# GpSimd normalises attention probabilities in four per-head pieces and takes their low parts in two halves

## The chip, the cores and the metric

The kernel runs on one core of one Trainium2 chip. The metric is the device time of one execution in microseconds (us); lower is better. Engine names as in the profile: PE is TensorE (matmuls), PEld its weight loads, DVE is VectorE, ACT is ScalarE, POOL is GpSimd, SP is SyncE, which here only issues DMAs.

## The reference

One transformer block on 16 independent sequences of 128 tokens and 512 channels: layer norm, cross-attention against a context of 128 positions and 128 channels (16 query heads, 4 key/value heads, rotary embedding, causal mask), a residual, layer norm, and a feed-forward with 4-bit weights and low-rank corrections. Cut to what matters:

```python
q = _rms_norm(q, q_norm_w); k = _rms_norm(k, k_norm_w)        # heads of 32, rotary on both
scores = jnp.einsum('bgnqd,bgkd->bgnqk', qg, k) * scale
scores = jnp.where(causal, scores, -1e+30)
attn = jax.nn.softmax(scores, axis=-1)                         # 16 heads, 128 x 128 each
out = jnp.einsum('bgnqk,bgkd->bgnqd', attn, v) ... @ w_out.T
x = x + out
y1 = ln(x) @ w_up + b_up + ln(x) @ w_up_lora_a @ w_up_lora_b   # 512 -> 2048
y2 = relu(y1) @ w_down + b_down + ...                          # 2048 -> 512
return x + y2
```

## The kernel before, in words

All matrices are held as a high and a low part in float16, and a product is three matmuls (high by high, low by high, high by low). A sequence ("batch" n, 16 of them) goes through: statistics, centring, rotary products (DVE, POOL, ACT), the split of queries and keys, their DMA transposes, scores on PE, and then the softmax in four tiles m = 0 to 3 of four heads each, 128 partitions by 512 columns:

- DVE masks the scores of a tile and takes the row maxima (`mask_and_max`, L1203), ACT takes exponentials and row sums (`exponentials`, L691, L696), and DVE takes the reciprocals of the four row sums (L1111).
- POOL multiplies the tile `pr[:, m]` (four heads of 128 columns) by the four reciprocals `rinv`, one per head and partition, in a single instruction (`probabilities`, L506), and signals `probs`.
- ACT rounds the tile to float16, the high part (L722), and signals `p_high`.
- POOL subtracts the high part from `pr[:, m]` in a single instruction, which gives the low part (`probabilities_low`, L515), and signals `p_low`.
- SP waits for both and issues the DMA transpose of the tile (L409) into `pT`. When all four tiles have landed, PE multiplies by the values (L907), and the output projection follows (L919).

The feed-forward of the batch then runs as four groups up (`feed_forward`, L937) and four parts down (L951). Between them DVE and ACT form `z`, `hid` and its low part (L1132, L756, L1141), and SP transposes them (L417). In the first fifth of the run the 4-bit weights are also unpacked: 32 tiles, scaled mostly by DVE (`dequant`, L1095; five by POOL, L476 and L479), turned on PE (L795, L848), split by ACT (L648) and DVE (L1103).

The order of the instructions on each engine is written out by hand. Time is cut in slots `s`, 264 of them to a batch, and tables `R_...` name the slot of each step for each engine; a step at batch n from 3 on repeats every 264 slots. A slot is no time: within one engine it is only the order, and between engines only semaphores tie. In a steady batch the order on POOL is: `values_low` (L521), `keys` (L489, L490, L493), `value_scales` (L529), probabilities of tiles 0 and 1, low part of tile 0, low part of tile 1, the power for the query and key norms (L498), `y` base (L555), probabilities of tile 2, the power for the second norm (L545), probabilities of tile 3, `cosines` (L538), low parts of tiles 2 and 3. On SP it is: keys, hidden part 0, queries, hidden part 1, probabilities tile 0, hidden parts 2 and 3, second norm (L394), probabilities tile 1, loads of a later batch, probabilities tiles 2 and 3, store.

Who waits for the touched steps: ACT's L722 waits for `probs` of its tile (L719), POOL's L515 for `p_high` (L514), SP's L409 for `p_high` and `p_low` (L405, L406), and DVE's L1203 of the next batch for `p_low` of the same tile (L1198), since it overwrites `pr[:, m]`.

Of the kernel before, what the change touches and what calls it, by code (L numbers as in the profile page):

```python
# [10 lines left out]
ALU = mybir.AluOpType  # L11
# [3 lines left out]
P = 128  # L15
# [92 lines left out]
def build(nc, x, ctx, qw, kw, wo, wuq, wus, bu, wua, wub, wdq, wds, bd, wda, wdb,  # L108
# [3 lines left out]
    HD, NG = 32, 4  # L112
# [16 lines left out]
    with ExitStack() as es:  # L129
# [16 lines left out]
        p3 = big[:, 6144:].bitcast(F16).rearrange("p (m g a t) -> p m g a t", m=NN, g=NG, a=2)  # L146
# [52 lines left out]
        pr = sb("pr", [P, NN, NG, P])  # L199
# [17 lines left out]
        rsum, rinv = sb("rsum", [P, 2, NN * NG]), sb("rinv", [P, 2, NN * NG])  # L217
# [50 lines left out]
        exps, inv_sums, probs = sem("exps"), sem("inv_sums"), sem("probs")  # L268
        sums_scaled, p_high, p_low = sem("sums_scaled"), sem("p_high"), sem("p_low")
# [48 lines left out]
        for s in range(SLOTS):  # L318
            n = at(s, R_VSUM)
            if n is not None:  # L320
                projs_before[n] = len(sums_before)
            n = at(s, R_PROJ)
            if n is not None:
                sums_before[n] = len(projs_before)
        for s in range(SLOTS):
# [5 lines left out]
            for g in range(4):  # L331
                n = at(s, R_UP[g])
# [4 lines left out]
                n = at(s, R_DOWN[g])  # L337
# [10 lines left out]
        def _(sp):  # L348
# [31 lines left out]
            for s in range(SLOTS):  # L380
                n = at(s, R_KTURN)
                if n is not None:
                    sp.wait_ge(k_low, n + 1)
                    sp.wait_ge(k_high, n + 1)
                    if n > 0:
                        sp.wait_ge(scores, 4 * n)
                    sp.dma_start_transpose(kT[:], k3[:].rearrange("p g a d -> p (g a d)")).then_inc(k_turned, 16)
                n = at(s, R_XNTURN)
                if n is not None:
                    sp.wait_ge(xn_high, n + 1)  # L390
                    sp.wait_ge(xn_low, n + 1)
                    if n > 0:
                        sp.wait_ge(up_done, 4 * n)
                    sp.dma_start_transpose(xnT[:], xn_parts[:].rearrange("p a c -> p (a c)")).then_inc(xn2_turned, 16)  # L394
                n = at(s, R_QTURN)
                if n is not None:
                    sp.wait_ge(q_low, n + 1)
                    sp.wait_ge(q_high, n + 1)
                    if n > 0:
                        sp.wait_ge(scores, 4 * n)  # L400
                    sp.dma_start_transpose(qT[:], q3[:].rearrange("p h a d -> p (h a d)")).then_inc(q_turned, 16)  # L401
                for m in range(NN):
                    n = at(s, R_PTURN[m])
                    if n is not None:
                        sp.wait_ge(p_high, 4 * n + m + 1)  # L405
                        sp.wait_ge(p_low, 4 * n + m + 1)  # L406
                        if n > 0:
                            sp.wait_ge(heads_out, n)
                        sp.dma_start_transpose(pT[:, m], p3[:, m].rearrange("p g a t -> p (g a t)")).then_inc(p_turned[m], 16)  # L409
                for g in range(4):  # L410
                    n = at(s, R_X2TURN[g])
                    if n is not None:
                        sp.wait_ge(x2_high, 4 * n + g + 1)
                        sp.wait_ge(x2_low, 4 * n + g + 1)
                        if n > 0:
                            sp.wait_ge(down_done, n)
                        sp.dma_start_transpose(x2T[:, g], hid[:, (4 * n + g) % HID_RING].rearrange("p a h -> p (a h)")).then_inc(x2_turned[g], 16)  # L417
                for g in range(1, 8):
                    if LOAD_AT[g - 1] == s:
                        load_group(g)  # L420
                for i, (parts, rows, moved) in enumerate(((b_up_parts, b_up3, b_up_rows), (b_dn_parts, b_dn3, b_dn_rows))):
                    if LORA_B_ROWS_AT[i] == s:
                        sp.wait_ge(b_high, 2)
                        sp.wait_ge(b_low, 2)
                        sp.wait_ge(lora_rows_empty, 4)
                        for j in range(3):
                            sp.dma_start(rows[R * j:R * j + R],
                                         parts[:, j, :]).then_inc(moved, 16)
                for n in (1, 2, 3):
                    if BATCH_LOAD_AT[n - 1] == s:  # L430
                        load_batch(n)
                if s == LORA_D_LOAD_AT:
                    sp.dma_start(a_nat[:, KC * R:].rearrange("p (g a) -> p g a", a=4 * R), wda_v).then_inc(a_dn_in, 16)
                if s == WO_LOAD_AT:
                    sp.dma_start(wo_raw, wo.rearrange("(j p) c -> p j c", p=P)).then_inc(wout_in, 16)
                if s == ROW_LOAD_AT:
                    sp.dma_start(b_row[:], bu.rearrange("(a n) -> a n", a=1).broadcast_to([P, H])).then_inc(bias_row_in, 16)
                if s == DOWN_BIAS_LOAD_AT:
                    sp.dma_start(bd_bc[:], bd.rearrange("(a n) -> a n", a=1).broadcast_to([P, C])).then_inc(down_bias_in, 16)
                n = at(s, R_STORE)  # L440
                if n is not None:
                    store(n)
                n = at(s, R_LOAD)
                if n is not None and n + RING < B:
                    load_batch(n + RING)
# [4 lines left out]
        def _(pool):  # L450
# [49 lines left out]
            def probabilities(s):  # L500
                for m in range(NN):
                    n = at(s, R_PROBS[m])
                    if n is not None:
                        p = n % 2
                        pool.wait_ge(inv_sums, 4 * n + m + 1)
                        pool.tensor_tensor(pr[:, m], pr[:, m],  # L506
                                           rinv[:, p, 4 * m:4 * m + 4].unsqueeze(2).broadcast_to([P, NG, P]),
                                           ALU.mult).then_inc(probs, 1)

            def probabilities_low(s):  # L510
                for m in range(NN):
                    n = at(s, R_PLOW[m])
                    if n is not None:
                        pool.wait_ge(p_high, 4 * n + m + 1)  # L514
                        pool.tensor_tensor(p3[:, m, :, 1, :], pr[:, m], p3[:, m, :, 0, :], ALU.subtract).then_inc(p_low, 1)  # L515

            def values_low(s):
                n = at(s, R_VLOW)
# [67 lines left out]
        def _(act):  # L586
# [112 lines left out]
            def attention(s):  # L699
                n = at(s, R_SQUARES)  # L700
                if n is not None:
                    act.wait_ge(kv_in[n % RING], 16 * (n // RING + 1))
                    if n >= 2:
                        act.wait_ge(v_summed, n - 1)
                    act.activation(sq_junk[:], kvt[:, n % RING, :], ACT.Square,
                                   accum_out=ssq[:, n % 2:n % 2 + 1]).then_inc(ctx_sq, 1)
                n = at(s, R_KSPLIT)
                if n is not None:
                    act.wait_ge(norms, n + 1)
                    act.wait_ge(k_ready, n + 1)  # L710
                    if n > 0:
                        act.wait_ge(k_turned, 16 * n)
                    act.activation(k3[:, :, 0:2, :], k[:].rearrange("p (g d) -> p g d", d=HD).unsqueeze(2)
                                   .broadcast_to([P, NG, 2, HD]), ACT.Identity,
                                   scale=inv[:, n % 2, 1:2]).then_inc(k_high, 1)
                for m in range(NN):
                    n = at(s, R_PHIGH[m])
                    if n is not None:
                        act.wait_ge(probs, 4 * n + m + 1)  # L719
                        if n > 0:  # L720
                            act.wait_ge(p_turned[m], 16 * n)
                        act.activation(p3[:, m, :, 0, :], pr[:, m], ACT.Copy).then_inc(p_high, 1)  # L722
                n = at(s, R_VSPLIT)
                if n is not None:
                    act.wait_ge(v_scaled, n + 1)
                    if n > 0:
                        act.wait_ge(heads_out, n)
                        act.wait_ge(v_low, n)
                    act.activation(vs[:], kvt[:, n % RING, :], ACT.Identity,
                                   scale=v_scales[:, n % 2, 0:1]).then_inc(v_sized, 1)  # L730
                    act.wait_ge(v_sized, n + 1)
                    act.activation(v3[:, 0, :], vs[:], ACT.Copy).then_inc(v_high, 1)
# [244 lines left out]
        def _(dve):  # L977
# [213 lines left out]
            def mask_and_max(s):  # L1191
                for m in range(NN):
                    n = at(s, R_MASK[m])
                    if n is not None:
                        p = n % 2
                        dve.wait_ge(scores, 4 * n + m + 1)
                        if n > 0:
                            dve.wait_ge(p_low, 4 * n + m - 3)  # L1198
                        if n == 0 and m == 0:
                            dve.wait_ge(consts_in, 16)  # L1200
                        for g in range(NG):
# [127 lines left out]
```

## Time and profile before

| what | value |
|---|---|
| time, median of 3 runs | 485.31 us (483.17 to 486.15) |
| the profiled execution | 484.46 us |
| its span, first to last instruction | 482.7 us |
| PE busy | 443.0 us, 92% |
| DVE busy | 352.0 us, 73% |
| ACT busy | 300.3 us, 62% |
| POOL busy | 282.1 us, 58% |
| L506, 64 instructions of 128x512 | 72.7 us, mean 1137 ns |
| L515, 64 instructions of 128x512 | 80.9 us, mean 1272 ns |
| mean granted TensorE clock | 0.979 of full |

The busy share of an engine is an average over stages with different limits. The profiled execution's own 484.46 us holds 1.8 us outside its span, and is 0.85 us under the median of the three runs.

### The profile page before, as it was taken

To read this page: it belongs to the slowest core of one execution; us is meant where nothing else is said; L and a number is where in the kernel's file an instruction comes from. 1 tells how busy PE (TensorE), PEld (TensorE's weight loads), DVE (VectorE), ACT (ScalarE), POOL (GpSimd) and SP (SyncE) were. 2 spreads that over 40 slices of the span, in tenths; PEclk is the share of its full clock that TensorE was granted. 3 is DMA by queue.
4 is the path that set the end of the run, shared out by engine and by line. 5 is a ranking of instruction groups with operands and counts; after the bars stand their busy time and mean duration, and the time that the engine had idled before them with its cause. 6 is when DMAs were issued, how large, how long until landed. Compare 5 with 4: busy or idle time off the path is not lost.

```text
span 482.7 us, 8285 instructions
## 1 busy us (share of the span) xinstructions
PE 443.0 (92%) x2416; PEld 218.2 (45%) x2416; DVE 352.0 (73%) x1076; ACT 300.3 (62%) x927; POOL 282.1 (58%) x304
## 2 busy tenths in 40 slices
PE   0285869999999999999999999999999999999997
PEld 0164545444444444444444444444444445444443
DVE  3899998979879786868686877778777856534341
ACT  1698978878858675757575757666675856422120
POOL 5477767685859574848384747576657745451100
PEclk9996879999999999999999999999999999999999
DMA  8679769789777858887867777897697777474422
GB/s 224 215 245 175 189 206 209 114 167 141 160 121 137 168 109 160 135 171 114 171 130 155 134 158 132 169 132 161 122 135 163 118 153 110 91 125 93 88 56 74
DMA packets 207740, 70.36 MB, mean 146 GB/s; under 512 B 196880, under 2 KB 200096, under 8 KB 207056
## 3 DMA queue, kind: packets, MB, share of 16 engines
q1 hardware_dynamic: 206864, 69.35, 72.7%
q8 instruction: 19, 0.31, 0.3%
q10 hardware_dynamic: 752, 0.34, 0.3%
q0 software_dynamic: 80, 0.16, 0.2%
q14 instruction: 25, 0.20, 0.1%
HBM read 17.15 MB, written 4.19 MB: 44 GB/s over the span
## 4 chain that ended last, share of the span: by engine, by line
PE 78%; DVE 1%; DMA 1%; SPq 0%; issue 0%
PE ff L951 33%; PE ff L937 33%; PE tb L919 8%; PE sb L891 2%; PE tb L907 2%; DMA x<-hid 1%; SPq L401 0%; PE tb L877 0%; DVE t_sin L1171 0%; DVE pr L1203 0%; DVE y L1253 0%; DVE stats L1184 0%; DVE x L1181 0%; DVE q L1212 0%; DVE q L1118 0%
## 5 line engine op out<-in xcount | busy, mean ns | idle before, releaser
L951 PE MATMUL ff<-wd_hi,x 128*128 128x512 f16 x512 | 152.3, 379 | 0.7 <-DMA x<-hid 0.7
L937 PE MATMUL ff<-wu_hi,xnT 128*128 128x512 f16 x512 | 152.7, 380 | 0.0
L691 ACT ACTIVATE pr<-pr,nmax 128x128 f32<-128x128 f32 x256 | 99.0, 389 | 13.6 <-DVE nmax L1203 12.9
L515 POOL TENSOR_TENSOR big<-pr,big 128x512 f16<-128x512 f32 x64 | 80.9, 1272 | 32.6 <-ACT big L722 32.6
L937 PE MATMUL ff<-wu_lo,xnT 128*128 128x512 f16 x256 | 97.0, 379 | 0.0
L951 PE MATMUL ff<-wd_lo,x 128*128 128x512 f16 x256 | 97.0, 379 | 0.0
L506 POOL TENSOR_TENSOR pr<-pr,rinv 128x512 f32<-128x512 f32 x64 | 72.7, 1137 | 35.6 <-DVE rinv L1111 35.6
L756 ACT ACTIVATE hid<-z 128x512 f16<-128x512 f32 x64 | 39.9, 624 | 80.1 <-DVE z L1132 80.1
L1203 DVE CUSTOM_DVE_ANT_0 pr<-sb,tabs,score_scale 128x128 f32<-128x128 f32 x256 | 73.8, 344 | 12.3 <-PE sb L891 11.2
L937 PEld LDWEIGHTS ff<-wu_hi,xnT 128*128 128x128 f16 x512 | 48.2, 98 | 58.4 <-issue 5.9
L1132 DVE SCALAR_TENSOR_TENSOR z<-ff,su,b_row 128x512 f32<-128x512 f32 x64 | 47.7, 745 | 36.0 <-PE ff L937 34.7
L951 PEld LDWEIGHTS ff<-wd_hi,x 128*128 128x128 f16 x512 | 48.6, 98 | 52.9 <-DMA x<-hid 0.8
L1141 DVE SCALAR_TENSOR_TENSOR hid<-z,hid 128x512 f16<-128x512 f32 x64 | 48.0, 750 | 23.6 <-ACT hid L756 23.0
L722 ACT ACTIVATE big<-pr 128x512 f16<-128x512 f32 x64 | 39.7, 620 | 20.3 <-POOL pr L506 20.3
L691 ACT ACTIVATION_READ_ACCUMULATOR pr<-pr,nmax 128x1 f32 x256 | 48.1, 188 | 0.0
L937 PEld LDWEIGHTS ff<-wu_lo,xnT 128*128 128x128 f16 x256 | 25.0, 98 | 30.4 <-issue 0.3
L951 PEld LDWEIGHTS ff<-wd_lo,x 128*128 128x128 f16 x256 | 25.0, 97 | 30.3
L489 POOL TENSOR_TENSOR k_cos<-kvt,cwk 128x128 f32<-128x128 f32 x16 | 8.2, 513 | 48.1 <-DMA kvt<-in_ctx 44.9
L555 POOL TENSOR_TENSOR y<-x,bd_bc 128x512 f32<-128x512 f32 x16 | 20.8, 1299 | 14.4 <-DMA out<-y 14.4
L1224 DVE SCALAR_TENSOR_TENSOR oT_lo<-tb,oT_hi 128x512 f16<-128x512 f32 x16 | 11.1, 691 | 22.6 <-ACT oT_hi L680 22.6
L680 ACT ACTIVATE oT_hi<-tb 128x512 f16<-128x512 f32 x16 | 9.5, 596 | 28.7 <-PE tb L907 28.7
L891 PE MATMUL sb<-kT,qT 96*128 96x128 f16 x256 | 24.9, 223 | 1.8 <-DVE nmax L1203 1.8
(144 smaller groups left out, 652.7 us busy)
## 6 DMA issues: line engine op xcount, KB each, us to landing
xt<-in_x SPq DMA_DIRECT2D x16, 256.0 KB, 3.0
big<-in_L_ffn_w_up_q SPq DMA_DIRECT2D x4, 1024.0 KB, 7.3
big<-in_L_ffn_w_down_q SPq DMA_DIRECT2D x4, 1024.0 KB, 6.2
out<-y SPq DMA_DIRECT2D x16, 256.0 KB, 2.7
wd_lo<-in_L_xattn_w_out SPq DMA_DIRECT2D x1, 1024.0 KB, 7.5
pT<-big SPq DMA_TRANSPOSE x64, 3.5
b_row<-in_L_ffn_b_up SPq DMA_DIRECT2D x1, 1024.0 KB, 9.1
x<-hid SPq DMA_TRANSPOSE x64, 3.2
```

The lines of the kernel that those rows point to most:

```text
L506: pool.tensor_tensor(pr[:, m], pr[:, m], rinv[:, p, 4 * m:4 * m + 4].unsqueeze(2).broadcast_to([P, NG, P]), ALU.mult).then_inc(probs, 1)
L515: pool.tensor_tensor(p3[:, m, :, 1, :], pr[:, m], p3[:, m, :, 0, :], ALU.subtract).then_inc(p_low, 1)
L691: last = act.activation(pr[:, m, g, :], pr[:, m, g, :], ACT.Exp, bias=nmax[:, p, j:j + 1], scale=-1.0, accum_out=rsum[:, p, j:j + 1])
L722: act.activation(p3[:, m, :, 0, :], pr[:, m], ACT.Copy).then_inc(p_high, 1)
L756: act.activation(hid[:, (4 * n + g) % HID_RING, 0, :], z[:, g % 2], ACT.Relu).then_inc(x2_high, 1)
L891: last = pe.matmul(sbk[m % 2][:, P * g:P * g + P], qT[0:HD3, 4 * m + g, :], kT[0:HD3, g, :], start=True, stop=True)
L919: last = pe.matmul(tb[0][:], a[:, m, :], b[:, m, :], start=(i == 0 and m == 0), stop=(i == 2 and m == NN - 1))
L937: last = pe.matmul(bank[:], a[:, m, :], b[:, m, 512 * g:512 * g + 512], start=(m == 0 and i == 0), stop=(m == KC - 1 and i == 2))
L951: last = pe.matmul(ff[down_bank[n]][:], x2T[:, part, k + h % HG, :], b[:, h, :], start=(h == 0 and i == 0), stop=(h == HC - 1 and i == 2))
L1132: dve.scalar_tensor_tensor(z[:, g % 2], ff[up_bank[n, g]][:], su[:], b_row[:, 512 * g:512 * g + 512], ALU.mult, ALU.add).then_inc(ff_read, 1)
L1141: dve.scalar_tensor_tensor(h[:, 1, :], z[:, g % 2], 0.0, h[:, 0, :], ALU.max, ALU.subtract).then_inc(x2_low, 1)
L1203: last = dve.tensor_tensor_reduce(pr[:, m, g, :], sbk[m % 2][:, P * g:P * g + P], mask, score_scale[:], 3e38, ALU.add, ALU.min, nmax[:, p, ...
```

## The change

The normalisation of a tile is no longer one `tensor_tensor` of 128x512 against a broadcast of four reciprocals, but four `tensor_scalar` of 128x128, one per head, each with the reciprocal of that head as its per-partition operand. The low part of a tile is two `tensor_tensor` of 128x256 where it was one of 128x512. Each piece signals, so `probs` counts four to a tile and `p_low` two to a tile, and the waits in SP, ACT and DVE are scaled to match: they still wait for the whole tile. No instruction changes its place among the others, and what is computed is the same.

```diff
@@ block.sync, p turn
-                        sp.wait_ge(p_low, 4 * n + m + 1)
+                        sp.wait_ge(p_low, 2 * (4 * n + m + 1))
@@ probabilities
-                        pool.tensor_tensor(pr[:, m], pr[:, m],
-                                           rinv[:, p, 4 * m:4 * m + 4].unsqueeze(2).broadcast_to([P, NG, P]),
-                                           ALU.mult).then_inc(probs, 1)
+                        for h in range(NG):
+                            pool.tensor_scalar(pr[:, m, h, :], pr[:, m, h, :], rinv[:, p, 4 * m + h:4 * m + h + 1], None,
+                                               ALU.mult).then_inc(probs, 1)
@@ probabilities_low
-                        pool.tensor_tensor(p3[:, m, :, 1, :], pr[:, m], p3[:, m, :, 0, :], ALU.subtract).then_inc(p_low, 1)
+                        pool.tensor_tensor(p3[:, m, 0:2, 1, :], pr[:, m, 0:2], p3[:, m, 0:2, 0, :], ALU.subtract).then_inc(p_low, 1)
+                        pool.tensor_tensor(p3[:, m, 2:4, 1, :], pr[:, m, 2:4], p3[:, m, 2:4, 0, :], ALU.subtract).then_inc(p_low, 1)
@@ block.scalar, high part
-                        act.wait_ge(probs, 4 * n + m + 1)
+                        act.wait_ge(probs, 4 * (4 * n + m + 1))
@@ mask_and_max
-                            dve.wait_ge(p_low, 4 * n + m - 3)
+                            dve.wait_ge(p_low, 2 * (4 * n + m - 3))
```

## Rows read from the trace of the kernel before

**Rows 1.** Chain that ended last: start us, us, what; from 93 us to the end.

```profile
93.53 1.38 DVE t_sin L1171
...
100.78 3.17 DMA x<-hid
...
104.00 2.76 PE ff L951 x12
...
289.38 0.76 PE tb L907 x12
...
314.60 0.76 PE tb L907 x12
...
479.41 0.75 DVE y L1253
```

**Rows 2.** Busy time by stage: window, us, busy per engine (instructions), clock, DMA share, GB/s.

```profile
40.00:80.00 40.00, 31.62 (x170) 20.42 (x171) 38.26 (x107) 34.89 (x102) 28.02 (x27) 0.76 0.87 199
...
304.00:329.00 25.00, 25.00 (x139) 11.73 (x137) 18.71 (x60) 16.38 (x54) 15.78 (x18) 1.00 0.84 145
```

**Rows 3.** POOL by line: count, duration ns min/median/max, first and last start, form.

```profile
L506 POOL TENSOR_TENSOR pr<-pr,rinv x64: 1033/1041/1566, 34.5 to 425.1; 128x512 f32<-128x512 f32 x64
...
L515 POOL TENSOR_TENSOR big<-pr,big x64: 1148/1162/1615, 41.4 to 427.6; 128x512 f16<-128x512 f32 x64
...
L476 POOL TENSOR_SCALAR big<-big x5: 619/941/1119, 31.6 to 83.2; 128x512 f32<-128x512 int32 x5
...
L489 POOL TENSOR_TENSOR k_cos<-kvt,cwk x16: 454/458/784, 13.7 to 361.2; 128x128 f32<-128x128 f32 x16
...
L521 POOL TENSOR_TENSOR v<-vs,v x16: 422/426/878, 53.2 to 429.2; 128x128 f16<-128x128 f32 x16
```

**Rows 4.** Timeline of POOL, one steady batch: start us, us, instruction, [idle before].

```profile
302.02 2.71 POOL L515 TENSOR_TENSOR big<-pr,big 128x512 f16<-128x512 f32 x2
...
310.06 0.46 POOL L489 TENSOR_TENSOR k_cos<-kvt,cwk 128x128 f32<-128x128 f32 x1 [4.94 <-DMA kvt<-in_ctx]
...
322.58 1.49 POOL L506 TENSOR_TENSOR pr<-pr,rinv 128x512 f32<-128x512 f32 x1
```

**Rows 5.** Timelines of ACT, SP and PE in the same batch.

```profile
324.10 0.63 ACT L722 ACTIVATE big<-pr 128x512 f16<-128x512 f32 x1 [1.98 <-POOL pr L506]
...
303.78 1.23 SPq L394 DMA_TRANSPOSE xnT<-xn_parts  x1
...
307.60 2.62 SPq L409 DMA_TRANSPOSE pT<-big  x2
...
309.25 0.60 PE L937 MATMUL ff<-wu_hi,xnT 128*128 128x512 f16 x2
```

**Rows 6.** DMA issues: median us from issue to landing.

```profile
xnT<-xn_parts SPq DMA_TRANSPOSE x16, 3.2
```

**Rows 7.** Timelines of POOL and PE around batch 0's product with the values.

```profile
50.54 1.16 POOL L515 TENSOR_TENSOR big<-pr,big 128x512 f16<-128x512 f32 x1 [1.46 <-ACT big L722]
...
55.34 0.83 PE L907 MATMUL tb<-pT,v 128*32 128x512 f16 x12 [0.52 <-issue]
```

**Rows 8.** Timelines of POOL and DVE around 93 us.

```profile
93.19 1.16 POOL L515 TENSOR_TENSOR big<-pr,big 128x512 f16<-128x512 f32 x1
...
93.45 1.45 DVE L1171 TENSOR_TENSOR t_sin<-xc,sw 128x512 f32<-128x512 f32 x1
```

**Rows 9.** DVE's L1095: its spread of durations, then four places of its timeline.

```profile
L1095 DVE SCALAR_TENSOR_TENSOR big<-big,s_dn x12: 660/683/1650, 52.8 to 87.3; 128x512 f32<-128x512 int32 x12
...
45.93 2.14 DVE L1095 SCALAR_TENSOR_TENSOR big<-big,s_up 128x512 f32<-128x512 int32 x2
...
55.69 2.11 DVE L1095 SCALAR_TENSOR_TENSOR big<-big,s_dn 128x512 f32<-128x512 int32 x2
...
66.56 1.64 DVE L1095 SCALAR_TENSOR_TENSOR big<-big,s_dn 128x512 f32<-128x512 int32 x1
...
79.84 1.65 DVE L1095 SCALAR_TENSOR_TENSOR big<-big,s_dn 128x512 f32<-128x512 int32 x1
```

## The prediction

> **What bounds the kernel now.** I read the chain that ended last first [rows 1]. Before 104 us it runs through DVE instructions and transposes; from 104.00 to 479.4 us it is PE alone, one matmul group behind another, and only the last DVE instruction stands behind it. The same group, L907, returns at 289.38 and at 314.60, so a batch takes 25.22 us of PE without a gap. The busy times by stage [rows 2] say the same: in the window 304 to 329, which is nearly one batch, PE is busy for 25.00 of 25.00 us and POOL for 15.78, so POOL has 9.2 us to spare in a batch. In the window 40 to 80 it is another kernel: DVE is busy for 38.26 of 40 us, PE for 31.6, POOL for 28.0. So there are two questions. Does POOL, with its new instructions, stay hidden behind PE from 104 us on? And does the stretch before 104 us, which DVE bounds, get shorter or longer? What happens there moves the whole rest of the run one for one.
>
> **What the change costs on POOL.** *Normalisation.* A tile was one instruction of 1.04 us (median) [rows 3]. It becomes four `tensor_scalar` of 128x128 with a per-partition operand, a form that this trace doesn't have. The nearest rows bound one piece: from below a quarter of the one-input L476 of 128x512, 0.619 / 4 = 0.155 us, as if an instruction had no fixed part; from above the two-input L489 of 128x128, 0.458 us (0.784 at its worst, when it shares its time with DVE). I take the middle, 0.31 us. A tile then costs 4 x 0.31 = 1.24 us, +0.20; the ends are 0.62 (-0.42) and 1.83 (+0.79). *Low part.* L515 takes 1.162 us for 512 columns, L521, the same operation with the same types, 0.426 for 128. That is (1.162 - 0.426) / 384 = 1.92 ns a column and 0.18 us fixed, so a half of 256 columns takes 0.67 us and two take 1.34: +0.18. No change at all (0.0) is the lower end, two L521's fixed parts more (+0.36) the upper. *Sum.* A batch has four tiles: 4 x (0.20 + 0.18) = +1.5 us on POOL, from 15.8 to 17.3 us in 25.22. The upper ends give 4 x (0.79 + 0.36) = +4.6, to 20.4. Both fit.
>
> The Trainium skill speaks against the change here: its page GPSIMD Engine Reference, in the section on performance pitfalls for Q7 kernels, says that each small read command costs about 102 cycles that do not overlap with the one before, which at the 1.2 GHz of that page is an estimated 85 ns. If the fetch of the per-head operand were such a command, a piece would be 0.31 + 0.085 = 0.40 us and a tile +0.54 in place of +0.20. No run here shows it yet; the forecast would stay as it is.
>
> **Does it stay hidden in the steady batches?** Three places. *(a) POOL as a whole*: it stands idle for 4.94 us ahead of L489, waiting for the context DMA [rows 4], and that gap takes up all that was late in the batch. *(b) The third tile.* ACT waits 1.98 us for exactly this normalisation (POOL 322.58, ACT 324.10 [rows 4, 5]), so what it grows by goes straight into ACT's high part, and behind that on ACT, without a gap, the second norm, whose low part DVE takes before SP issues the transpose at 303.78 [rows 5] (one batch earlier in the trace). It lands 3.2 us later [rows 6], at 307.0, and PE uses it at 309.25 [rows 5]: 2.3 us of cover against +0.2, at most +0.8. *(c) Tiles 2 and 3's low parts*: from the third tile on POOL runs without a gap until 304.73 (302.02 + 2.71 [rows 4]), and SP issues the first of their two transposes at 307.60 [rows 5], 2.9 us later. Added ahead of it are two normalisations and two low parts, 2 x 0.20 + 2 x 0.18 = 0.8 us, 2.3 at the upper ends. DVE's wait for `p_low` is for the batch before, and DVE is busy for only 18.7 of 25 us there. So from 104 us on I put the whole change at nothing; what hides it is PE's 25.22 us a batch. The scaled waits cost nothing either: they release when the last piece of the same tile is done.
>
> **The stretch before 104 us.** *What gets later.* The product with the values in batch 0 starts at 55.34 us after a pause, 3.6 us after the fourth low part ends at 51.70 [rows 7]. Ahead of this low part POOL was idle for 1.46 us, waiting for ACT, so longer normalisations vanish in that gap and only the two halves count: +0.18 us. DVE works without a gap there and doesn't wait for it directly, so I take +0.2 for batch 0 and batch 1 together and +1.0 as the upper end (all growth of two tiles at the upper bounds of the normalisation, less what the gap absorbs).
>
> *What gets earlier.* DVE and POOL block one another. At 93.19 POOL starts a low part of 1.16 us; at 93.45 DVE starts L1171, with both inputs in SBUF, and needs 1.45 us for what takes 0.68 undisturbed: it ends 0.55 us after POOL's instruction does, as if it had stood still until then [rows 8]. 1.38 us of it stand in the chain [rows 1]. L1095 is 0.68 us by its median and 1.65 at worst [rows 9]. The four places there, less what they take alone (0.68 for one, 1.28 for two in a row), lose 0.86 and 0.83 us beside normalisations, and 0.96 and 0.97 beside low parts. With L1171's 0.77 that is 1.69 us lost to normalisations and 2.70 to low parts, on the engine that bounds this stretch. If DVE gets its turn at the end of POOL's current instruction, shorter instructions shorten the stall. A normalisation piece ends after 0.31 us at most, so the two stalls keep some 0.25 each and 1.2 us come back; a half ends 0.49 us sooner than the whole (1.16 - 0.67), so three stalls give 1.5 back. Of these 2.7 us I let half reach 104 us, 1.35, since PE, ACT and SP have waits of their own between. POOL is busy longer, which makes new collisions: +0.1. Bounds: all 2.7 arrive, or none, where DVE loses its turn to the next piece.
>
> **The sum**, against the profiled execution's own 484.46 us: +0.2 (later turns) - 1.35 (shorter stalls) + 0.1 (new collisions) + 0.0 (steady) = -1.05, so 483.4. The median of the runs stands 0.85 above the profiled execution; on that scale it is 485.3 - 1.05 = 484.3 us. A measurement of this kernel can tell about 1% from no change, 4.9 us; this isn't that.
>
> **The rivals.** *Rival 1, POOL pieces are expensive (slower).* Place: the normalisation, 16 pieces a batch. It decides where a piece of price p fills POOL's spare time: 16p - 4 x 1.04 + 0.7 = 9.2, so p = 0.79 us; at (b) the limit is 4p - 1.04 = 2.3, p = 0.83. Above it PE waits in each batch. At p = 1.0 a batch is 15.8 - 4.2 + 16 + 0.7 = 28.3 us long, +3.1, and about twelve full batches (104 us to the end of the attention work at about 425) give +37: 522 us. For it: a form that the trace doesn't show, and the 0.784 us that a two-input 128x128 once took. Against: the one-input 128x512 takes 0.62 us in all, so 1.0 for a quarter of the columns would need a fixed part that no row has. Chance 7%.
>
> *Rival 2, no lock relief.* DVE's stalls stay, since POOL's next piece is ready as soon as the last has ended, and more pieces give more collisions. What is left is the lateness: +0.2 to +1.5, so 485.5 to 486.8. For it: POOL's instructions follow one another within 0.04 us. Against: in rows 8 DVE runs as soon as POOL's instruction is over. Chance 30%.
>
> *Rival 3, the relief arrives in full* and DVE's start-up loses 2.7 us or more, since 4.4 us of such stalls are there: 481 to 482.5. Chance 12%, and 4% more that the gain passes 1%, if other places that I didn't list ease too.
>
> My own case, 483 to 485.5, has the remaining 47%. Rival 1 between the two regimes (p of 0.6 to 0.8, only the start-up late) is within the 30% of rival 2. Adding noise of about 1 us: faster by over 1% 5%, within 1% 87%, slower by over 1% 8%. The range for 8 in 10 takes in rivals 2 and 3 and leaves out rival 1: 481.3 to 487.5.
>
> **What would show it.** In the profile after: L506 with 256 instructions of about 0.31 us; L515 with 128 of about 0.67; POOL busy near 282 + 64 x 0.38 = 306 us; PE without a gap from about 103 us on, again 25.22 us a batch; the stretch before that shorter by about 1 us, with the worst L1095 under 1.3 us in place of 1.65. ACT's waits for L506 would grow from 1.98 to about 2.2 us at tile 2. I would be wrong if a piece takes over 0.8 us or PE shows waits in steady batches (rival 1), and wrong in the start-up if L1095 and L1171 still take up to 1.6 us and PE's unbroken run starts later than 104 us (rival 2).

## The result, and the profile after

The changed kernel takes 499.05 us (median of 4 runs, 497.74 to 500.5) where the kernel before takes 485.6 (median of 4). The ratio is 1.0289, 95% interval 1.0257 to 1.0321: 13.5 us slower. The profiled execution took 497.74 us with a span of 496.0, so the two traces differ by 13.3 us.

The head of the page of the kernel after, and its costliest POOL groups (columns as in the page: line, engine, operation, tiles, form, count, busy us, mean ns, idle before and what ended it):

```profile
PE 444.5 (90%) x2416; PEld 218.3 (44%) x2416; DVE 355.3 (72%) x1076; ACT 303.1 (61%) x927; POOL 389.4 (79%) x560
...
L507 POOL TENSOR_SCALAR pr<-pr,rinv 128x128 f32<-128x128 f32 x256 | 168.6, 676 | 11.8 <-DVE rinv L1112 11.8
...
L515 POOL TENSOR_TENSOR big<-pr,big 128x256 f16<-128x256 f32 x64 | 54.3, 848 | 1.3 <-ACT big L723 1.3
...
L516 POOL TENSOR_TENSOR big<-pr,big 128x256 f16<-128x256 f32 x64 | 44.8, 701 | 0.0
```

PE does the same work as before, 444.5 us, in a longer span. POOL's busy time has grown by 107 us, from 282.1 to 389.4: the normalisation grew by 96 (72.7 to 168.6) and the low parts by 18 (80.9 to 99.1), while its other work took some 3 us less; the rest of the difference is that the records of neighbouring instructions overlap at their edges, which total busy time counts once. The spread of the touched lines of the kernel after (duration ns min/median/max) answers to [rows 3]:

```profile
L507 POOL TENSOR_SCALAR pr<-pr,rinv x256: 597/605/1518, 34.0 to 440.3; 128x128 f32<-128x128 f32 x128
...
L515 POOL TENSOR_TENSOR big<-pr,big x64: 662/676/1180, 42.2 to 442.4; 128x256 f16<-128x256 f32 x64
...
L516 POOL TENSOR_TENSOR big<-pr,big x64: 659/672/1219, 42.8 to 443.0; 128x256 f16<-128x256 f32 x64
```

A half costs what was forecast, 0.67 us, by its median; by their means, with the time lost beside DVE, two halves take 1.55 us where the whole took 1.27, +0.28 in place of +0.18. A normalisation piece costs 0.605, twice the 0.31 of the forecast, and above the upper end of its range: four quarters take 2.42 us where the whole took 1.04.

The chain that ended last, in the kernel after, is no longer PE alone. One batch of it (start us, us, what), from one load of the context to the next:

```profile
344.80 2.78 DMA kvt<-in_ctx
...
349.05 0.68 POOL v_scales L530
349.73 5.23 POOL pr L507 x8
354.95 0.64 POOL big L515
...
358.16 1.24 POOL y L556
359.40 1.36 POOL pr L507 x2
...
362.74 0.62 ACT hid L757
...
365.36 1.70 DVE xn_parts L1233
367.12 1.23 SPq L394
...
368.77 1.24 SPq L409
...
370.69 3.02 DMA kvt<-in_ctx
```

Read it as a loop. POOL can't start the keys of the next batch before their context has landed. SP issues that load behind the transposes of the second norm and of probability tile 1. The second norm comes from DVE, whose input ACT makes behind the high part of tile 2, and that waits for POOL's third normalisation. So POOL's own lateness comes back to POOL through SP's queue. A turn of the loop takes 25.89 us here (344.80 to 370.69). PE's product with the values, from batch 6 to batch 12, comes every 25.58 to 25.98 us. PE needs 25.22.

Where the 13.3 us arise can be read from the start of PE's product with the values, L907 before and L908 after, batch by batch: batch 2 starts at 115.37 before and at 119.68 after (+4.3), batch 12 at 364.97 and 376.22 (+11.3), batch 13 at 390.19 and 403.46 (+13.3), and the distance stays to the end. So 4.3 us are lost up to batch 2, and 9.0 from there to batch 13. The 9.0 aren't spread evenly: 3.7 arise between batches 2 and 6 (1.9 of them from 5 to 6), 3.2 in the six turns from 6 to 12, and 2.0 from 12 to 13. PE's two longest pauses from 104 us on are in the timeline of PE in the kernel after:

```profile
119.68 0.83 PE L908 MATMUL tb<-pT,v 128*32 128x512 f16 x12 [2.20 <-issue]
...
398.18 0.61 PE L938 MATMUL ff<-wu_hi,xnT 128*128 128x512 f16 x2 [1.62 <-DMA xnT<-xn_parts]
```

### The profile page after: what moved, and what is told of

It is laid out like the page before. It is cut to its first block, busy times and chain, and to the rows that moved or that the text cites. A ratio compares the mean times of both kernels' runs of the same rounds, so it can differ in the third digit from the quotient of the medians.

```text
span 496.0 us, 8541 instructions
## 1 busy us (share of the span) xinstructions
PE 444.5 (90%) x2416; PEld 218.3 (44%) x2416; DVE 355.3 (72%) x1076; ACT 303.1 (61%) x927; POOL 389.4 (79%) x560
## 4 chain that ended last, share of the span: by engine, by line
POOL 34%; PE 19%; DMA 6%; DVE 6%; SPq 6%; issue 4%; ACT 1%; ACTq 0%; DVEq 0%; POOLq 0%
POOL pr L507 18%; PE ff L938 8%; PE ff L952 8%; DMA kvt<-in_ctx 5%; POOL big L516 3%; DVE xn_parts L1233 3%; POOL y L556 3%; POOL big L515 3%; SPq L409 2%; SPq L394 2%; DVE pr L1204 2%; PE tb L920 2%; POOL inv L498 2%; POOL v_scales L530 1%; SPq L353 1%
## 5 line engine op out<-in xcount | busy, mean ns | idle before, releaser
L507 POOL TENSOR_SCALAR pr<-pr,rinv 128x128 f32<-128x128 f32 x256 | 168.6, 676 | 11.8 <-DVE rinv L1112 11.8
L1142 DVE SCALAR_TENSOR_TENSOR hid<-z,hid 128x512 f16<-128x512 f32 x64 | 50.1, 784 | 44.5 <-ACT hid L757 43.8
L515 POOL TENSOR_TENSOR big<-pr,big 128x256 f16<-128x256 f32 x64 | 54.3, 848 | 1.3 <-ACT big L723 1.3
L516 POOL TENSOR_TENSOR big<-pr,big 128x256 f16<-128x256 f32 x64 | 44.8, 701 | 0.0
L1233 DVE SCALAR_TENSOR_TENSOR xn_parts<-xn,inv,xn_parts 128x512 f16<-128x512 f32 x16 | 21.6, 1353 | 8.1 <-ACT xn_parts L747 8.1
L489 POOL TENSOR_TENSOR k_cos<-kvt,cwk 128x128 f32<-128x128 f32 x16 | 8.6, 537 | 23.3 <-DMA kvt<-in_ctx 22.3
L1225 DVE SCALAR_TENSOR_TENSOR oT_lo<-tb,oT_hi 128x512 f16<-128x512 f32 x16 | 11.1, 691 | 21.6 <-ACT oT_hi L681 21.5
```

Of the source, the lines that this page charges most:

```text
L507: pool.tensor_scalar(pr[:, m, h, :], pr[:, m, h, :], rinv[:, p, 4 * m + h:4 * m + h + 1], None, ALU.mult).then_inc(probs, 1)
L515: pool.tensor_tensor(p3[:, m, 0:2, 1, :], pr[:, m, 0:2], p3[:, m, 0:2, 0, :], ALU.subtract).then_inc(p_low, 1)
L516: pool.tensor_tensor(p3[:, m, 2:4, 1, :], pr[:, m, 2:4], p3[:, m, 2:4, 0, :], ALU.subtract).then_inc(p_low, 1)
L1142: dve.scalar_tensor_tensor(h[:, 1, :], z[:, g % 2], 0.0, h[:, 0, :], ALU.max, ALU.subtract).then_inc(x2_low, 1)
L1233: dve.scalar_tensor_tensor(xn_parts[:, 1, :], xn2[:], inv2[:, n % 2:n % 2 + 1], xn_parts[:, 0, :], ALU.mult, ALU.subtract).then_inc(xn_low, 1)
```

## The experiments

All ratios are against runs of the kernel before on the same chip; in the four groups of runs behind the experiments its median is 483.9 to 484.1 us.

**e1, only the halves.**

```diff
-  pool.tensor_tensor(p3[:, m, :, 1, :], pr[:, m], p3[:, m, :, 0, :], ALU.subtract).then_inc(p_low, 1)
+  pool.tensor_tensor(p3[:, m, 0:2, 1, :], pr[:, m, 0:2], p3[:, m, 0:2, 0, :], ALU.subtract).then_inc(p_low, 1)
+  pool.tensor_tensor(p3[:, m, 2:4, 1, :], pr[:, m, 2:4], p3[:, m, 2:4, 0, :], ALU.subtract).then_inc(p_low, 1)
```

> Only the low part is taken in two halves; the normalisation is one instruction a tile, as before. Theory (the loss is the normalisation's 16 pieces a batch at 0.68 us each): no loss; the halves cost POOL 64 x 0.3 = 19 us of busy time in its spare 9 us a batch, so within 1% of before, 483.5 to 487 us. Rival (each extra POOL instruction costs a fixed amount whatever it does, so halves carry a share by their number, 64 of 256 extra instructions): +3.4 us, 489. Second question: shorter low parts shorten DVE's stalls in L1095, from up to 1.65 us to about 1.2, which should start PE's unbroken run up to 1 us earlier.

Measured: 483.55 us, ratio 0.999 (0.9974 to 1.0007). The halves cost nothing; the loss isn't a matter of the number of instructions. The worst L1095 (L1096 here) is still 1.535 us, beside an undivided normalisation. The gain that I expected from shorter stalls isn't clear of noise.

**e2, only the normalisation pieces.**

```diff
-  pool.tensor_tensor(pr[:, m], pr[:, m], rinv[...4 columns...].unsqueeze(2).broadcast_to([P, NG, P]), ALU.mult)
+  for h in range(NG):
+      pool.tensor_scalar(pr[:, m, h, :], pr[:, m, h, :], rinv[:, p, 4 * m + h:4 * m + h + 1], None, ALU.mult)
```

> Only the normalisation is in four tensor_scalar pieces; the low part is one instruction a tile. Theory: nearly the whole loss of 13.5 us is here: 496 to 499 us, L506's successor at 0.60 us median a piece. Rival (loss by number of POOL instructions, 192 of 256 extra ones): 496. Rival (the two edits only exceed POOL's spare time together): under 490 us.

Measured: 494.13 us, ratio 1.0203 (1.0185 to 1.0221), a piece at 0.600 us. So 10 of the 13.5 us are here, less than the "nearly the whole" of the theory, whose 496 to 499 us were missed, and as many as the rival by number of instructions gave; e1 rules that rival out, and so does e3 below, with 192 more instructions at no cost. The halves cost nothing alone and some 3 us on top of the pieces: once POOL's slack is used up, their 0.2 us a tile counts.

**e3, pieces in the old form.**

```diff
+  for h in range(NG):
+      pool.tensor_tensor(pr[:, m, h, :], pr[:, m, h, :],
+                         rinv[:, p, 4 * m + h:4 * m + h + 1].broadcast_to([P, P]), ALU.mult)
```

> The normalisation is in four pieces of 128x128 as in the change, but each is a tensor_tensor against the broadcast reciprocal, the form of before; low part whole. It separates the splitting from the form. Theory A (the per-partition operand of tensor_scalar is what is dear): a piece 0.36 to 0.43 us, like a quarter of 1.04 plus 0.18 fixed, 1.6 us a tile in place of 2.42, and the time returns to 485 to 488 us. Rival (any POOL instruction of 128x128 costs 0.6 us here, because pr and p3 or the semaphore make it so): a piece 0.6 us and 496 to 499 us.

Measured: 484.18 us, ratio 1.0008 (0.9994 to 1.0022). The spread of this kernel's pieces:

```profile
L507 POOL TENSOR_TENSOR pr<-pr,rinv x256: 392/398/940, 34.2 to 427.3; 128x128 f32<-128x128 f32 x128
```

0.398 us for the same product on the same tile, against 0.605 for `tensor_scalar`. Splitting in four is free here; the form of the pieces is what cost.

**e4, the changed kernel with its loads earlier on SP.**

```diff
-R_LOAD = (1595, 1631, 2016, 2307)
+R_LOAD = (1595, 1631, 2016, 2237)
```

> The changed kernel, with the loads of a later batch moved on SP ahead of the second norm's transpose from batch 3 on. In the changed kernel POOL waits 22 us for the context DMA, which SP issues behind the transposes that wait for DVE's second norm, which wait through ACT for POOL's third tile: a loop of 25.6 us a batch. Theory (this loop, not POOL's own sum of 23 us, sets the steady batches): POOL's waits for kvt fall under 5 us, the batch returns to 25.22 and of the 13.5 us lost about 9 (those after 120 us) come back: 489 to 492 us. Rival (POOL is simply full, its busy time and its waits for rinv and arg2 fill 25.6 us): 498 to 500 us, with the waits for kvt turned into others.

Measured: 492.23 us, ratio 1.0157 (1.0135 to 1.0178) against before. The loss has gone from 13.5 to 8.2 us, so 5.3 have come back (5.1 between the two traces) and not the 9 that I expected; the time lies 0.2 us beyond the slow end of the range. POOL's waits for the context are down from 22.3 to 0.8 us. PE's product with the values starts at 195.88, 221.10, 246.32 and so on to 372.42 us in batches 5 to 12, 25.22 apart, though the pieces take 0.60 us as before. The first and the last of them, in the timeline of PE of e4:

```profile
195.88 0.83 PE L908 MATMUL tb<-pT,v 128*32 128x512 f16 x12
...
372.42 0.83 PE L908 MATMUL tb<-pT,v 128*32 128x512 f16 x12
```

The loop through SP's queue, not POOL's sum, bounded these steady batches. What remains is +5.1 us at batch 2, 2.4 more from batch 2 to 5 and 0.8 from 12 to 13; why they remain wasn't tried.

**e5, e6, e13, e14: what a piece is made of.** Each leaves out part of the computation, as its expectation says.

```diff
+ e5   pool.tensor_scalar(pr[:, m, h, :], pr[:, m, h, :], 2.0 ** 7, None, ALU.mult)             # 4 a tile
+ e13  pool.tensor_scalar(pr[:, m, h, :], pr[:, m, h, :], 2.0 ** 7, 1.0, ALU.mult, ALU.mult)    # 4 a tile
+ e6   pool.tensor_scalar(pr[:, m], pr[:, m], rinv[:, p, 4 * m:4 * m + 1], None, ALU.mult)      # 1 a tile
+ e14  pool.tensor_scalar(pr[:, m], pr[:, m], rinv[:, p, 4 * m:4 * m + 1], 1.0, ALU.mult, ALU.mult)
```

> Four tensor_scalar pieces of 128x128 as in the change, but each multiplies by a constant written into the instruction in place of the reciprocal in SBUF; this leaves out the division by the row sum. Low part whole. Theory A (fetching the per-partition operand is what is dear): a piece about 0.30 us, near half of 0.60, and 483.5 to 486 us. Rival B (tensor_scalar has a high fixed cost on POOL whatever its operand): 0.55 to 0.60 us a piece and 493 to 495 us.

> One tensor_scalar of 128x512 a tile with the reciprocal of the tile's first head as its operand; this leaves out the other three heads' own reciprocals. It splits the price of a piece in a fixed and a per-column part. If the operand is fetched once (theory A1): 0.60 + 384 columns at 0.8 ns = 0.91 us, a fixed part of about 0.5 us, and the time of before. If it costs in every column (theory A2): 4 x 0.60 less little, over 2.0 us, and 490 us or more.

> As e5, constants in the instruction in place of the reciprocals (the division by the row sum is left out), but with two operations, as L476 has, and still on a float input. Theory (two operations are the fast form): 0.25 to 0.30 us a piece, 482 to 485 us. Rival (the integer input made L476 fast): 0.53 us as in e5, or more, and 487 to 489 us. If e12 is slow and this one fast, the operand in SBUF is what keeps a piece from the fast form.

> As e6, one tensor_scalar of 128x512 a tile with the first head's reciprocal (the other heads' own reciprocals are left out), now with the second operation of e12. It shows whether the second operation acts on each column or once an instruction. Theory (one operation costs 2.5 ns a column, two cost 0.84): 0.374 + 384 x 0.84 ns = 0.70 us, in place of 1.57, and 482 to 485 us. Rival (the second operation only saves a fixed 0.23 us): 1.34 us, and the same time.

Spread of durations of the normalisation line, of e5:

```profile
L507 POOL TENSOR_SCALAR pr<-pr x256: 518/527/1033, 34.5 to 429.8; 128x128 f32<-128x128 f32 x128
```

of e6:

```profile
L506 POOL TENSOR_SCALAR pr<-pr,rinv x64: 1557/1572/2437, 33.8 to 423.6; 128x512 f32<-128x512 f32 x64
```

of e13:

```profile
L507 POOL TENSOR_SCALAR pr<-pr x256: 289/297/795, 33.6 to 424.2; 128x128 f32<-128x128 f32 x128
```

and of e14:

```profile
L506 POOL TENSOR_SCALAR pr<-pr,rinv x64: 683/691/1677, 34.0 to 423.4; 128x512 f32<-128x512 f32 x64
```

e5 and e6 contradicted both of my theories in turn. A constant in place of the operand in SBUF saves only 0.073 us (0.600 in e2, 0.527 in e5), so the fetch isn't what is dear. That is rival B's side of e5, though the piece came out just under B's 0.55 and the time well under its 493. And e6 came out between A1 and A2: 1.572 us, (1.572 - 0.600) / 384 = 2.53 ns a column, far more than L476's 0.62 us for all 512. That left one visible difference besides the integer input: L476 carries two operations. e13 confirms it: with two operations 0.297 us, on a float input, where e5 with one takes 0.527. e14 shows that it acts in each column: 0.691 us for 512, and (0.691 - 0.374) / 384 = 0.83 ns a column, with e12's 0.374 for 128 columns. The times: e5 487.74 us, 1.008 (1.0053 to 1.0107); e6 483.31, 0.9988 (0.9971 to 1.0005); e13 483.2, 0.9991 (0.9972 to 1.0011); e14 482.81, 0.9984 (0.996 to 1.0007).

e5 is also a test of the loop: with 0.527 us a piece, PE's product with the values keeps its 25.22 us from 191.47 to 418.45. Its loss of 3.8 us arises earlier. With the low part whole, as in e5, 0.600 us is about the point from which steady batches get longer: in e2 most still take 25.22, and two between batches 6 and 12 take 25.85 and 25.82.

**e9 and e10: where in the run the pieces hurt.**

```diff
+ e9   if n >= 3: (four tensor_scalar) else: (one tensor_tensor); loads early as in e4, low part whole
+ e10  if n < 3:  (four tensor_scalar) else: (one tensor_tensor); loads as before, low part whole
```

> The dear pieces from batch 3 on only, the loads early as in e4; batches 0 to 2 normalise in one instruction, low part whole everywhere. Theory (of e4's remaining loss of 8 us about 4.5 arise in batches 0 to 2 and the rest at their seam): PE's product with the values of batch 2 starts at 115 to 116 us as before, and steady batches take 25.22: 484 to 487 us. Rival (the remaining loss is in the steady batches): 490 to 492 us.

> The complement: pieces in batches 0 to 2 only, 48 of 256, everything else as before, loads too. Theory: PE's product with the values of batch 2 starts 3.5 to 4.5 us later than before and nothing is added or won back afterwards: 487.5 to 489.5 us. Rival (late starts are absorbed, since steady batches have cover): under 486 us.

Measured: e9 485.75 us, ratio 1.0046 (1.0023 to 1.0069); e10 488.95, ratio 1.0107 (1.0085 to 1.0129). In e10 the product with the values starts at 119.68 in batch 2 and at 443.89 in batch 15, 4.3 us late both times (115.37 and 439.58 before): 48 dear pieces cost 5 us and nothing absorbs them. In e9, 208 dear pieces with the loads early cost 1 us in the trace (440.54 in batch 15) and 1.8 by the medians. So once the loads are early, the start-up is the dearer place by far. In the changed kernel itself, with its loads late, the batches behind it cost 9.0 us and the start-up 4.3.

**e12, the changed kernel with two operations in each piece.**

```diff
-  pool.tensor_scalar(pr[:, m, h, :], pr[:, m, h, :], rinv[:, p, 4 * m + h:4 * m + h + 1], None, ALU.mult)
+  pool.tensor_scalar(pr[:, m, h, :], pr[:, m, h, :], rinv[:, p, 4 * m + h:4 * m + h + 1], 1.0, ALU.mult, ALU.mult)
```

> The changed kernel whose normalisation pieces carry a second operation, a multiplication by the constant 1.0, as the kernel's own tensor_scalar at L476 (add, then multiply by 1.0) does; results are the same. One-operation pieces cost 0.60 us for 128 columns and 1.57 for 512, so 2.5 ns a column and 0.28 us fixed, while L476 takes 0.62 us for 512 columns. Theory (POOL treats tensor_scalar with one operation worse than with two): a piece 0.28 to 0.35 us, a tile 1.2 us, DVE's stalls short, and 482 to 485 us. Rival (L476 is fast for its integer input or its constants): a piece stays at 0.60 us or is slower, 497 to 502 us.

Measured: 482.44 us (12 runs), ratio 0.9972 (0.9956 to 0.9987). One added multiplication by 1.0 takes back the whole loss and 1.4 us more. A piece costs a little more than the 0.28 to 0.35 us of the theory:

```profile
L507 POOL TENSOR_SCALAR pr<-pr,rinv x256: 366/374/1322, 34.7 to 425.7; 128x128 f32<-128x128 f32 x128
```

**e11, both splits, with `tensor_tensor` pieces.**

> The change's split of both steps, with the normalisation pieces as tensor_tensor against the broadcast reciprocal (0.40 us each in e3). It leaves every touched POOL instruction under 0.7 us. Theory of relief (DVE gets its turn at the end of POOL's current instruction, and the start-up passes it on): 1 to 2 us under before, 482 to 483.5 us. Rival (relief is used up by the longer sum on POOL): 484 to 486 us.

Measured: 482.62 us (12 runs), ratio 0.9975 (0.996 to 0.9991). It and e12 have intervals clear of 1; e1 and e3, which split one step each, have not. But all of these intervals overlap, so no gain of both splits over one is shown. Both runs are the change as it was meant, with cheap pieces.

## Why the prediction was wrong

**The price of a piece** is the step that failed first. I bounded it by a quarter of L476 (0.155 us) and by L489 (0.458), and took 0.31; it is 0.605. Both ends were rows of other instructions: L489 is a `tensor_tensor`, and L476 is a `tensor_scalar` with two operations. I noted that L476 has one input and overlooked that it has two operations, add and multiply by 1.0, where the change's pieces have one. Two operations would have made my number nearly right: 0.374. The growth of POOL by "+1.5 us a batch, +4.6 at the upper ends" was 107 / 16 = 6.7.

The estimate of 85 ns for the fetch of the per-head operand, and of 0.40 us a piece, stood beside the sum. The fetch costs 0.600 - 0.527 = 0.073 us in the slow form and 0.374 - 0.297 = 0.077 in the fast one, so the fetch isn't what made the piece dear. The Trainium skill's page GPSIMD Engine Reference, in the section on performance pitfalls for Q7 kernels, gives about 102 cycles for a small read command, an estimated 85 ns at the 1.2 GHz of that page, and doesn't say that such an operand is one; these rows are near its figure, which doesn't prove that it is the reason.

**The steady batches.** I named three places with 9.2, 2.3 and 2.9 us of cover and put rival 1's threshold at 0.79 us a piece. Steady batches got longer at 0.605, so the threshold was wrong too. The mistake is in place (a): I counted POOL's 4.94 us ahead of L489 [rows 4] as a gap that "takes up all that was late". It doesn't, for it is ended by the context DMA, and SP issues that behind the second norm's transpose, so the end of the gap moves with POOL's lateness. What absorbs is only the idle time on the way round the loop. The timeline of POOL in the kernel before shows it between the keys and the third normalisation of a batch:

```profile
314.36 1.04 POOL L506 TENSOR_TENSOR pr<-pr,rinv 128x512 f32<-128x512 f32 x1 [1.22 <-DVE rinv L1111]
316.89 1.16 POOL L515 TENSOR_TENSOR big<-pr,big 128x512 f16<-128x512 f32 x1 [1.50 <-ACT big L722]
318.65 1.16 POOL L515 TENSOR_TENSOR big<-pr,big 128x512 f16<-128x512 f32 x1 [0.60 <-ACT big L722]
320.70 0.69 POOL L498 TENSOR_TENSOR inv<-arg,minus_half 128x2 f32<-128x2 f32 x1 [0.88 <-DVE arg L1160]
```

That is 1.22 + 1.50 + 0.60 + 0.88 = 4.2 us of waits. The rest of the way, from the end of the third normalisation to the next keys, takes 11.2 us before and 11.1 after, so it gave almost nothing. The same stretch of the kernel after has none of these waits:

```profile
322.05 0.46 POOL L489 TENSOR_TENSOR k_cos<-kvt,cwk 128x128 f32<-128x128 f32 x1 [2.50 <-DMA kvt<-in_ctx]
...
324.12 5.25 POOL L507 TENSOR_SCALAR pr<-pr,rinv 128x128 f32<-128x128 f32 x8
329.35 0.67 POOL L515 TENSOR_TENSOR big<-pr,big 128x256 f16<-128x256 f32 x1
...
331.86 0.72 POOL L498 TENSOR_TENSOR inv<-arg,minus_half 128x2 f32<-128x2 f32 x1
332.55 1.27 POOL L556 TENSOR_TENSOR y<-x,bd_bc 128x512 f32<-128x512 f32 x1
333.80 2.79 POOL L507 TENSOR_SCALAR pr<-pr,rinv 128x128 f32<-128x128 f32 x4
```

Two tiles take 5.25 us for 2 x 1.04 (+3.2), the four halves 2.5 for 2.3 (+0.2), the third tile 2.79 for 1.49 (+1.3): 4.7 us of growth against 4.2 us of cover, 0.5 too much, and a turn of 25.6 to 25.9 us against PE's 25.22. By the same sum a piece may cost an estimated 0.57 us, between e5 (0.527, no loss in steady batches) and the change. And e4, which takes the load out of the loop, brings 25.22 back with POOL busy for 23.8 us of 26 (window 330 to 356). So POOL's own sum wasn't yet the limit at 0.60 us a piece; whether it becomes one at 0.79, no run shows. Another limit came first. This reading covers the 3.2 us of the six steady turns; how much of the 5.8 around them is the same loop isn't shown.

**The start-up.** Two steps of opposite sign. *The relief of DVE* came at L1095, and there even beyond its number. DVE's L1095 (L1096 after) between 30 and 104 us, first in the kernel before:

```profile
L1095 DVE SCALAR_TENSOR_TENSOR big<-big,s_dn 128x512 f32<-128x512 int32 x12 | 11.9, 1002 | 0.0
L1095 DVE SCALAR_TENSOR_TENSOR big<-big,s_up 128x512 f32<-128x512 int32 x7 | 6.1, 914 | 0.1
```

then after:

```profile
L1096 DVE SCALAR_TENSOR_TENSOR big<-big,s_dn 128x512 f32<-128x512 int32 x12 | 8.7, 736 | 0.0
L1096 DVE SCALAR_TENSOR_TENSOR big<-big,s_up 128x512 f32<-128x512 int32 x7 | 4.9, 740 | 0.0
```

18.0 us became 13.6, so 4.4 us of stall are gone from these 19 instructions, with a worst case of 0.95 us where it was 1.65. But L1171 (L1172 after), whose stall I had read in the chain, got no relief: it takes 1.69 us at 94.35 where it took 1.45, now beside POOL's `t_cos` (L539, 94.21 to 95.49), which the change doesn't split. The next one is far worse. The timelines of DVE and POOL in the kernel after:

```profile
112.55 3.93 DVE L1172 TENSOR_TENSOR t_sin<-xc,sw 128x512 f32<-128x512 f32 x1
...
115.25 0.68 POOL L516 TENSOR_TENSOR big<-pr,big 128x256 f16<-128x256 f32 x1
```

It starts beside a low part (L515 at 112.14) and ends 0.55 us after the fifth POOL instruction in a row has ended (115.25 + 0.68 = 115.93). So DVE doesn't always get its turn at the end of POOL's current instruction, which was the condition of my relief and is what rival 2 doubted. A `hid` of DVE loses in the same way at 198.10: 3.17 us beside four halves in a row, just where the turn from batch 5 to 6 gets 1.9 us longer; that one causes the other wasn't tried. The 0.1 us that I had for new collisions was too small, and over the whole run DVE is busy for 3.3 us more than before (355.3 for 352.0).

*The lateness was wrong.* I had "+0.2, +1.0 as the upper end" for batches 0 and 1 and nothing for batch 2, and it is what gave 4.3 us of loss despite the relief. The product with the values is 0.9 us late in batch 0, 1.8 in batch 1 and 4.3 in batch 2. On POOL the four pieces of batch 1's second tile (from 63.51 us) stand ahead of the power for batch 0's second norm, and ACT waits for that once, and DVE for ACT. In batch 2 ACT waits for the normalisations. Among the waits of the stretch 60 to 125 us in the kernel after are

```profile
ACT big L723 <- POOL pr L507: 5.3, 4, 1.8
ACT xn_parts L747 <- POOL inv L546: 2.8, 1, 2.8
...
DVE xn_parts L1233 <- ACT xn_parts L747: 2.3, 1, 2.3
```

and then batch 2's product waits 2.20 us (above) for the last low part of its batch: it ends at 115.93 us on POOL, where the kernel before has finished it at 109.48. The low part comes 6.4 us later and the product 4.3 (115.37 and 119.68), so only 2.1 us were covered. DVE waits more: between 40 and 104 us it is busy for 56.4 us with 162 instructions, before for 61.3 with 169. e10 isolates the early batches: 5 us from 48 pieces.

Whether the relief alone gives something is not settled. In e12 and e11, where pieces are short and cheap, the gain is 1.4 and 1.2 us by the ratios, near the 1.05 us of the prediction's sum, and the worst L1095 are 1.16 and 1.22 us. But e6 and e14 leave the normalisation in one instruction, their worst L1095 is still 1.65 us, and their traces too have batch 2's product at 113.86 and 113.66 us, for 113.16 in e11, 114.47 in e12 and 115.37 before; their ratios, 0.9988 and 0.9984, have intervals that overlap with those of e11 and e12. So shorter stalls at L1095 are shown, and that they are what gave the gain is not. That the size agrees may be luck.

**The rivals.** Rival 1 had the right cause (pieces too dear) at 7%, and a wrong threshold, so its price, that of a POOL that is simply full, wasn't what came. Rival 2, at 30%, had DVE losing its turn right for some places (above), and its 485.5 to 486.8 us had the same small lateness as my own case. "Rival 1 between the two regimes" was put with rival 2 as harmless; that is where the kernel was. "What would show it" asked for PE waits in steady batches as the sign of rival 1, and that is what the trace shows.

**Left open.** Why POOL runs one operation slower than two was not found out: the runs show the price, not the cause. When DVE gets its turn between two POOL instructions and when it doesn't is open too. How the 4.3 us up to batch 2 divide among its three waits wasn't tried one by one, and neither was what makes the 3.7 us between batches 2 and 6 and the last 2.0 between 12 and 13.

## What to carry to other kernels

Price an instruction by a row with the same number of operations and the same kinds of operands; "same engine, same opcode" isn't enough, and when none exists the range must reach past the neighbours. An idle gap is cover only if what ends it doesn't hang on the engine's own earlier work: follow the releaser of the gap, a load here, back through the queue that issues it, and add up the idle time round the whole loop. Short pieces on GpSimd can shorten VectorE's stalls where both read SBUF. But pieces that follow one another without a gap can also hold VectorE over several of them, and if together they cost much more than the whole, the lateness outweighs the relief.

## What the runs showed of the hardware that I had not expected

Medians of GpSimd instructions on float tiles, us (L476 has an integer input):

| form | 128x128 | 128x512 |
|---|---|---|
| `tensor_scalar`, one operation, constant | 0.527 (e5) | |
| `tensor_scalar`, one operation, operand in SBUF | 0.605 (after), 0.600 (e2) | 1.572 (e6) |
| `tensor_scalar`, two operations, constants | 0.297 (e13) | 0.619 at least (L476, before) |
| `tensor_scalar`, two operations, operand in SBUF and constant | 0.374 (e12) | 0.691 (e14) |
| `tensor_tensor` against a broadcast column | 0.398 (e3) | 1.041 (before, four columns) |

A second operation that does nothing makes `tensor_scalar` 1.6 times as fast at 128 columns and 2.3 times at 512. With it, it is the fastest of these forms; without it, the slowest.

GpSimd and VectorE hold SBUF against each other by whole instructions: where VectorE's instruction started second, it lost the rest of GpSimd's [rows 8], and the worst L1095 fell from 1.65 to 0.95 us when GpSimd's became short. It can lose more than one: 3.93 us at 112.55 beside five GpSimd instructions in a row, 3.17 at 198.10 beside four, both in the kernel after. The Trainium skill's page SBUF — State Buffer, in the section on who interferes with whom, says that a VectorE instruction with two inputs in SBUF contends with a GpSimd instruction that reads SBUF, and calls this contention an exclusive lock; the rows agree [rows 8].
